# The scaled product of three ternary weight matrices moved to GpSimd, with more staging places and the third weight's sums in the first stage, in an attention and ternary feed-forward layer on eight cores

## The reference, cut to what matters

```python
def _weight_quant(w):
    scale = 1.0 / jnp.clip(jnp.mean(jnp.abs(w)), 1e-05)
    wq = jnp.clip(jnp.round(w * scale), -1.0, 1.0) / scale
    return w + jax.lax.stop_gradient(wq - w)
def _bitlinear(x, w):
    return jnp.einsum('bsi,oi->bso', _act_quant(x), _weight_quant(w))
...
qkv = grouped_linear(x, w_qkv, None)            # 8 groups of 128 channels
q, k, v = (qkv[0] * scale, qkv[1], qkv[2])      # 16 heads of 64
attn = jax.nn.softmax(jnp.einsum('bhnd,bhmd->bhnm', q, k), axis=-1)
out = jnp.einsum('bhnm,bhmd->bhnd', attn, v)    # then projected by w_proj
...
x = _layernorm(x + attention(x))
gate = jax.nn.silu(_bitlinear(x, w_gate))       # w_gate, w_up 4096 x 1024
up = _bitlinear(x, w_up)
x = _layernorm(x + _bitlinear(gate * up, w_down))   # w_down 1024 x 4096
```

## Time and profile before

| | us |
|---|---|
| median of 3 runs | 1290.41 (1288.22 to 1415.11) |
| profiled execution, its own time | 1290.59 |
| its span, slowest core (core 4) | 1289.0 |
| spans of the eight cores | 1278.8 to 1289.0 |
| busy in it: PE, DVE, ACT, POOL | 1149.7, 911.7, 616.9, 117.4 |

### The profile page before, as it was taken

How to read it: one execution, slowest core, us unless ns; L and a number is a source line. 1 busy time by engine, 2 the same in 40 slices (tenths; PEclk the granted TensorE clock), 3 DMA queues, 4 the chain that set the end, 5 groups by cost and what they waited for, 6 DMA issues and landing times.

```text
span 1289.0 us, 17877 instructions; the slowest of 8 cores (1278.8 to 1289.0 us)
## 1 busy us (share of the span) xinstructions
PE 1149.7 (89%) x6465; PEld 455.1 (35%) x6502; DVE 911.7 (71%) x1797; ACT 616.9 (48%) x679; POOL 117.4 (9%) x146
## 2 busy tenths in 40 slices
PE   3888998884898886599999999999999999999997
PEld 0333333321333222233333333333444444444443
DVE  4878889977899874474664547353789777977774
ACT  3798998884454487555555555554011111110110
POOL 1222112220001000010010001000000000000000
PEclk8999999997899898799999999999999999999999
DMA  8999934569799757242323223020523333233313
GB/s 237 307 326 316 325 102 158 176 195 318 239 250 226 208 138 241 90 92 65 92 70 78 86 39 117 5 70 1 145 89 81 89 82 99 72 89 66 82 34 82
DMA packets 129031, 179.74 MB, mean 139 GB/s; under 512 B 90033, under 2 KB 90801, under 8 KB 128946
## 3 DMA queue, kind: packets, MB, share of 16 engines
q1 hardware_dynamic: 120050, 149.52, 41.1%
q0 software_dynamic: 8896, 29.08, 7.4%
HBM read 127.41 MB, written 30.93 MB: 123 GB/s over the span
## 4 chain that ended last, share of the span: by engine, by line
PE 66%; DVE 13%; DMA 12%; ACT 5%; issue 4%; SPq 0%; POOL 0%; DVEq 0%; ACTq 0%; POOLq 0%
PE ps L802 32%; PE ps L897 16%; DMA stage<-wu 6%; PE ps L553 6%; PE ps L571 6%; PE ps L578 5%; ACT P L559 4%; DMA stage<-wd 3%; DVE asum L417 2%; DVE G L434 1%; ACT G L430 1%; DMA stage<-wg 1%; DMA stage<-xT 1%; DVE wgq L440 1%; DVE h L814 1%
## 5 line engine op out<-in xcount | busy, mean ns | idle before, releaser
L559 ACT ACTIVATE P<-ps 128x1024 bf16<-128x1024 f32 x512 | 492.5, 1021 | 236.6 <-PE ps L553 234.9
L808 ACT ACTIVATE T<-ps,tsc 128x512 f32<-128x512 f32 x128 | 88.0, 687 | 376.3 <-PE ps L802 330.5
L802 PE MATMUL ps<-wgq,xqT 128*128 128x512 fp8e4 x1024 | 249.2, 383 | 15.2 <-DVE hm L840 5.2
L802 PE MATMUL ps<-wuq,xqT 128*128 128x512 fp8e4 x1024 | 250.0, 384 | 8.7 <-DVE h L814 8.6
L897 PE MATMUL ps<-wdq,hqT 128*128 128x512 fp8e4 x1024 | 229.9, 380 | 1.3 <-DVE wdq L440 1.3
L571 PE MATMUL ps<-P,onesb 128*64 128x512 bf16 x1024 | 206.3, 399 | 14.2 <-DVE DT L594 14.2
L553 PE MATMUL ps<-Q,K 64*128 64x512 bf16 x1024 | 175.0, 389 | 44.1 <-ACT P L559 34.7
L578 PE MATMUL ps<-P,V 128*64 128x512 bf16 x1024 | 199.9, 386 | 0.9 <-DVE RC L598 0.5
L802 PEld LDWEIGHTS ps<-wuq,xqT 128*128 128x128 bf16 x1024 | 97.0, 99 | 142.0 <-issue 35.3
L802 PEld LDWEIGHTS ps<-wgq,xqT 128*128 128x128 bf16 x1024 | 95.8, 98 | 144.9 <-issue 39.9
L897 PEld LDWEIGHTS ps<-wdq,hqT 128*128 128x128 bf16 x1024 | 97.4, 98 | 129.8 <-issue 17.8
(11 more groups left out here) (95 smaller groups left out, 703.1 us busy)
## 6 DMA issues: line engine op xcount, KB each, us to landing
stage<-wu SPq DMA_DIRECT2D x64, 512.0 KB, 12.2
stage<-wd SPq DMA_DIRECT2D x58, 512.0 KB, 5.5
stage<-wg SPq DMA_DIRECT2D x42, 512.0 KB, 19.1
stage<-xT SPq DMA_DIRECT2D x16, 512.0 KB, 13.6
XB<-x SPq DMA_DIRECT2D x16, 512.0 KB, 5.3
xp_s<-XB SPq DMA_DIRECT2D x16, 512.0 KB, 2.6
Y<-xp_s SPq DMA_DIRECT2D x16, 512.0 KB, 4.3
y<-Y SPq DMA_DIRECT2D x16, 512.0 KB, 2.6
```

What stands on the lines that cost most here:

```text
L559: exp_tok[i] = act.do(lambda e: e.activation(P_sb[i % 4][:, :], bank(sb, 2), AF.Exp, bias=-C0, scale=0.125), pv_tok.get(i - 4), t)
L802: tp = pe.do(lambda e, ic=ic, w=w, bk=bk: e.matmul(bank(bk), xqT[b][:, ic, :], W_sb[w][:, 8 * q + ic, sl], start=(ic == 0), stop=(ic == 7) ...
L808: ta = act.do(lambda e: e.activation(T[:, :], bank(gb), AF.Tanh, bias=0.0, scale=tsc[:, t:t + 1]), tp, T_free[k], sc_tok[t])
```

## The change

The first operation of all 96 ternary tiles goes to GpSimd: times the scale, times 1.0, into 8-bit integers that saturate. VectorE does the limits for all of them, as before, but two tiles later in its queue than the product is put into GpSimd's, so four `G1` buffers are used. In the credit, a tile now costs 0.75 (the limit alone). w_up's first 16 ternary tiles use 12 places, 0 to 7 and 18 to 21. The sums of w_down use places 0 to 7, with no hold; only places 22 to 29 are held, until step 230 of the first stage. The pace of the first stage is 0.62 throughout (0.3 from step 242, as before). The first stage has 252 steps in place of 256, and the other 4 go into the second. `AT` has two buffers, and its loads are issued one tile earlier. `RB` has one buffer.

```diff
-    AT = alloc("AT", [128, 8, 128], BF16)[0]
+    AT = [alloc(f"AT{i}", [128, 7, 128], BF16)[0] for i in range(2)]
-    G1 = [alloc(f"G1{i}", [128, 1024], I8)[0] for i in range(2)]
+    G1 = [alloc(f"G1{i}", [128, 1024], I8)[0] for i in range(4)]
-    RB = [alloc(f"RB{i}", [128, 512], F32)[0] for i in range(2)]
+    RB = alloc("RB", [128, 512], F32)[0]
...
-    order += [("tern", 1, k, k % 8, True) for k in range(16)]
-    order += [("tern", 0, k, k % 8, True) for k in range(22, 24)]
+    ring = list(range(8)) + [18, 19, 20, 21]
+    order += [("tern", 1, k, ring[k % 12], True) for k in range(16)]
+    order += [("tern", 0, 22, 4, True), ("tern", 0, 23, 5, True)]
...
-    ring = [0, 1] + list(range(22, 30))
-    order += [("sum", 2, k, ring[n % 10], True) for n, k in enumerate(rest)]
+    order += [("sum", 2, k, n % 8, True) for n, k in enumerate(rest)]
...
-            if hold[0] and w == 2:
+            if hold[0] and s_ >= 22:
                 return
...
             if kind == "sum":
+                while second:
+                    yield limit()
...
-            if w == 2:
-                t = act.do(lambda e, w=w, src=src, b=b: e.activation(
-                    G1[b][:, :], src[:, :], AF.Identity, bias=0.0, scale=wst[:, 8 * w + 2:8 * w + 3]),
-                    g1_tok[b], t_stat[w], load_tok.get(o))
-            else:
-                t = dve.do(lambda e, w=w, src=src, b=b: e.tensor_scalar(
-                    G1[b][:, :], src[:, :], wst[:, 8 * w + 2:8 * w + 3], 1.0, ALU.mult, ALU.min),
-                    g1_tok[b], t_stat[w], load_tok.get(o))
+            t = pool.do(lambda e, w=w, src=src, b=b: e.tensor_scalar(
+                G1[b][:, :], src[:, :], wst[:, 8 * w + 2:8 * w + 3], 1.0, ALU.mult, ALU.mult),
+                g1_tok[b], t_stat[w], load_tok.get(o))
             used(o, t)
+            second.append((w, k, b, t))
+            if len(second) > 2:
+                yield limit()
...
+    def limit():
+        w, k, b, t = second.popleft()
+        g1_tok[b] = dve.do(lambda e: e.tensor_scalar(
+            W_sb[w][:, k, :], G1[b][:, :], -1.0, 1.0, ALU.max, ALU.min, saturate=False),
+            t, t_qkv_last[0] if w == 2 else None)
+        t_tern[(w, k)] = g1_tok[b]
+        return 0.75, None
...
-            RC[:, :].rearrange("r (k c) -> r k c", c=1).broadcast_to([128, 16, 32])), t2, u_free[b])
+            RC[:, :].rearrange("r (k c) -> r k c", c=1).broadcast_to([128, 16, 32])), t2, u_free[1 - b])
...
-            pace = 0.55 if 0 not in t_red else 0.75 if ast[0] < 230 else 0.95
+            pace = 0.62
...
-    for i in range(0, 256, 2):
+    for i in range(0, 252, 2):
...
             load_at(0)
+            load_at(1)
+        if i == 230:
+            hold[0] = False
+            for s_ in range(22, 30):
+                stage_tok[s_] = t_qkv_last[0]
+            load_more()
...
-    load_at(1)
-    hold[0] = False
...
-                if t + 1 != 8:
-                    load_at(t + 1)
+                if t + 2 < 16 and (t + 2) // 8 == t // 8:
+                    load_at(t + 2)
...
         elif kind == "X":
-            need_weights(2, 31)
+            if t == 0:
+                for k in range(32):
+                    need_weights(2, k)
```

More of the change, by code:

```diff
@@ L145, in build @@
     AO7 = alloc("AO7", [128, 1024], BF16)[0]
-    AT = alloc("AT", [128, 8, 128], BF16)[0]
-    blo, _ = alloc("blo", [128, 1024], BF16, at=off[0] - 2048)
+    AT = [alloc(f"AT{i}", [128, 7, 128], BF16)[0] for i in range(2)]
+    blo, _ = alloc("blo", [128, 1024], BF16, at=off[0] - 3584)
     b3, _ = alloc("b3", [128, 1024], BF16)
@@ L328, in build @@
     t_red = {}
-    g1_tok = [None, None]
+    g1_tok = [None] * 4
     g1_n = [0]
@@ L425, in weight_ops @@
                 continue
-            b = g1_n[0] % 2
+            b = g1_n[0] % 4
             g1_n[0] += 1
-            if w == 2:
-                t = act.do(lambda e, w=w, src=src, b=b: e.activation(
-                    G1[b][:, :], src[:, :], AF.Identity, bias=0.0, scale=wst[:, 8 * w + 2:8 * w + 3]),
-                    g1_tok[b], t_stat[w], load_tok.get(o))
-            else:
-                t = dve.do(lambda e, w=w, src=src, b=b: e.tensor_scalar(
-                    G1[b][:, :], src[:, :], wst[:, 8 * w + 2:8 * w + 3], 1.0, ALU.mult, ALU.min),
-                    g1_tok[b], t_stat[w], load_tok.get(o))
-            used(o, t)
[L438 to L443, removed]
+            t = pool.do(lambda e, w=w, src=src, b=b: e.tensor_scalar(
+                G1[b][:, :], src[:, :], wst[:, 8 * w + 2:8 * w + 3], 1.0, ALU.mult, ALU.mult),
+                g1_tok[b], t_stat[w], load_tok.get(o))
+            used(o, t)
+            second.append((w, k, b, t))
+            if len(second) > 2:
+                yield limit()
+        while second:
+            yield limit()
+    second = deque()
+    def limit():
[5 more added lines that the diff above has]
+        return 0.75, None
     later = []
@@ L600, in norm @@
         t3 = dve.do(lambda e: e.transpose(
-            RB[b][:, :].rearrange("r (k c) -> r k c", c=32),
-            RC[:, :].rearrange("r (k c) -> r k c", c=1).broadcast_to([128, 16, 32])), t2, u_free[b])
+            RB[:, :].rearrange("r (k c) -> r k c", c=32),
+            RC[:, :].rearrange("r (k c) -> r k c", c=1).broadcast_to([128, 16, 32])), t2, u_free[1 - b])
         def mult():
@@ L606, in mult @@
                 ao7_tok[qc] = u_free[b] = pool.do(lambda e: e.tensor_tensor(
-                    AO7[:, 512 * qc:512 * qc + 512], U_sb[b][:, :], RB[b][:, :], ALU.mult),
+                    AO7[:, 512 * qc:512 * qc + 512], U_sb[b][:, :], RB[:, :], ALU.mult),
                     pool.sem.tok(), t3, u_done_of[u], ao7_free[qc])
@@ L611, in mult @@
             t4 = u_free[b] = pool.do(lambda e: e.tensor_tensor(
-                AO[b][:, :], U_sb[b][:, :], RB[b][:, :], ALU.mult),
+                AO[b][:, :], U_sb[b][:, :], RB[:, :], ALU.mult),
                 pool.sem.tok(), t3, u_done_of[u], ao_free[b])
@@ L685, in load_at @@
         b = t % 2
-        atl_tok[t] = pool.dma(sem(f"atl{b}"), AT[:, 0:7, :], at_s[t, :, 0:7, :], at_free[0],
+        atl_tok[t] = pool.dma(sem(f"atl{b}"), AT[b][:, :, :], at_s[t, :, 0:7, :], at_free[b],
                               *[at_tok[(p, t // 4)] for p in range(7)])
@@ L723, in proj_half @@
             g = 4 * hf + j
-            src = AT[:, g, :] if g < 7 else AO7[:, 128 * (t % 8):128 * (t % 8) + 128]
+            src = AT[b][:, g, :] if g < 7 else AO7[:, 128 * (t % 8):128 * (t % 8) + 128]
             tp = pe.do(lambda e, g=g, j=j, src=src: e.matmul(
@@ L735, in proj_half @@
             return
-        at_free[0] = tp
+        at_free[b] = tp
         if t == 3 or t == 7:
@@ L951, in build @@
             load_at(0)
+            load_at(1)
[4 more added lines that the diff above has]
+            load_more()
         if i in (242, 244):
             proj_half(0, i // 2 - 121)
+            if i == 244:
+                load_at(2)
         att_weights(None if i < 242 else 0.3)
@@ L964, in build @@
         bgstep(1.0)
-    load_at(1)
-    hold[0] = False
-    for s_ in range(22, 30):
-        stage_tok[s_] = t_qkv_last[0]
-    load_more()
     gu_on[0] = True
@@ L1005, in need_weights @@
                 run_later(force=True)
+                while totals:
+                    totals.pop()(7)
+            assert not wdone[0] or (w, k) in t_tern
     for kind, t in seq:
@@ L1017, in build @@
                 load_at(8)
+                load_at(9)
             proj_half(t, 0)
@@ L1031, in build @@
                 if t == 0 and oc == 7:
+                    while 2 not in t_red:
+                        credit[0] = 1.0
+                        weight_step(credit)
                     hqT_alias[0] = [stage_tok[6], stage_tok[7]]
```

## The result

The changed kernel takes 1312.9 us (median of 4 runs, 1310.6 to 1313.4) against 1289.3 for the kernel before: a ratio of 1.0187, 95% interval 1.0175 to 1.0200. The forecast was 1258, 2.5% faster. The loss is just inside the range, and has the other sign. One of the four runs of the kernel before (1415.1 us) was in the slower state that some executions of every kernel here show, and is left out of the ratio.

A forecast was written before the change was run, and what follows sets the result against it. The prediction took TensorE to set the end after 548 us, with gains only in the differently bound stretches before; +30 - 24 - 9 - 31 + 2 = -32 us from 1290.6 gave about 1258 us, range 1225 to 1315.

The forecast's parts named there:

- P1 no longer waits: -24: Start of the second stage: with AT in two buffers, tile 1's projection no longer waits for its AT load, saving 24 us.
- what is late next is xqT of tile 0 ... no wait of size: After P1: the next late input is xqT of tile 0, its VectorE work issued before step 252, so no sizeable wait.
- P1 to GU2: Second stage, three blocks and two projections: less VectorE work makes it 160 us in place of 169, -9.
- First stage: Attention's 252 steps: late sums (3 us) and product-limit exclusion (34 us) move its end from 302 to 332, +30.
- 163 + 3: First stage: the last of 64 sums at 163 us by pace, plus 3 us of delay because DMA is full.
- my bound of 12: First stage: upper end of the sums' delay, put at 3 us (0 to 12), DMA being full until 160 us.
- Wait before D0: Before the first w_down matmul: all of w_down is ready early, so the wait goes, -31 us (526 to 495).
- Four steps: Four attention steps moved out of the first stage cost 4 x 0.6 us of TensorE, +2 us.
- B: Rival: GpSimd's product is dear, 1.9 us, delaying first stage and second-stage products; 1331 us, 3% slower; chance 0.18.
- A: Rival: no exclusion of size between GpSimd and VectorE; the ternary stretch costs 7 us, not 34; 1231 us; chance 0.2.
- C: Rival: gain given back by larger first-stage delays and GU0 to GU1 still bound by VectorE; 1284 us; chance 0.17.

The follow-up runs named there:

- Experiment 4: The kernel before with AT in two buffers, its loads issued one tile earlier, and RB in one buffer, nothing else of the change: 1287.0 us, ratio 1.0002.
- experiment 3: The changed kernel with places 22 to 29 released at the end of the first stage (the late release) in place of step 230: 1299.2 us.
- Experiment 10: w_down's sums on ScalarE: in a row, on the kernel before with two AT buffers, 1311.9 us; one by one, second stage only, on experiment 6, 1282.7 us.
- experiment 5: Kernel before, two AT buffers, w_gate and w_up products on GpSimd: 1285.8 us. Changed kernel, products on VectorE and ScalarE, places 22 to 29 released late: 1288.6 us.
- experiment 1: A small kernel without the layer: eight GpSimd products and eight VectorE limits, alone, together, and with sums; one run, 97.4 us, no layer time.
- experiment 6: The changed kernel with places 22 to 29 released at the first stage's end and a ternary tile counted 1.1 in place of 0.75: 1281.4 us, ratio 0.9943.

## Why the prediction was wrong

**The step that failed is the one on AT: "P1 no longer waits: -24", with "what is late next is xqT of tile 0 ... no wait of size".** It measured +4 and is 28 us off; the step after it adds 18, and the two turn the sign. Experiment 4 shows the term at 0 in the kernel before: xqT of tile 0 landed only at 322.9, 4.5 us before GU0. VectorE's backlog that I named as the cause of GpSimd's late product was as much the cause of a late xqT, and I removed one of two waits of nearly equal length. In the changed kernel it came worse: the early release put loads ahead of the transfer of xqT (experiment 3, 13 us). I had checked the loads of AT against GpSimd's queue, and not SyncE's queue, where the change puts 34 loads ahead of that one transfer.

**P1 to GU2, -9, measured +9.** I took VectorE's 147 of 169 us for the bound and counted its work. Experiment 10 takes 30 us of that work away and gains 4 us in the stretch and none in the time. In the changed kernel VectorE is busy for only 86 of 110 us from 370 to 480. The chain there goes through products, transfers of w_down (18.9 us of GpSimd's idle time) and VectorE's limits, with the tanh products queued among them; so a part of the 31 us saved before D0 is paid here, one tile at a time. Of the 9 us, some 4 are there with the old engines and the late release too (171.4 us, experiment 5), and some 4 come with the products on GpSimd (175.2, experiment 3). The cores of one execution differ by up to 5 us in this stretch, so the parts are rough.

**First stage, +30, measured +39.** The mechanism was right, and nearly its rates: exclusion (experiment 1), 1.63 us for a tile in a row against 1.72 by the sum, 1.86 with all that comes between against 1.8, and the product's price, 1.11 against 1.07. The reading of two pairs of rows was enough for that. By the cited section of the Trainium skill ("SBUF — State Buffer", section "SBUF: two separate sides", there under "Who interferes with whom") VectorE's reductions never contend for the shared ports on this chip; the trace agrees, with sums every 1.14 us and products of 1.11 beside them (experiment 1).

That the size came so near is in part luck. Step 252 is over only at 350, not at 332: 18 us late. But the first stage of the kernel before ends at 316 and not at 302, which was step 242: 14 us the other way. Of the 18, ten are sums: the last of the 64 ended at 176 us in place of 163 + 3; DMA was full until 160, at 323 GB/s, and my bound of 12 was the better value. The rest is in the tiles (119 us in place of 115, 75 steps in place of 77). And the exclusion is not the whole of the delay. With both operations on the old engines and the late release P0 is 24 us late (experiment 5), and it is GpSimd that adds the other 11 or 12 (329.1 to 340.5, and 326.3 to 337.8). The 24 are work moved forward and come back before D0; what is lost for good is the engine's 11 and the transfers' 13 us.

**Wait before D0, -31: right. Four steps, +2:** from D0 on it measured -1; a term of this size can't be told apart.

**Rivals.** B (a dear product) is refuted by 1.11 to 1.13 us, though its 1331 is nearer to the measured time than the forecast. A is refuted by experiment 1. C is the nearest in what happened (the sums' ten us, and GU0 to GU2 no faster), but it has neither the transfer queue nor the late xqT, and says 1284.

**What costs, in the end.** The credit says 0.75 for a tile, which puts one in every 1.27 us, and product and limit need 1.63 together, so the order puts tiles in faster than they can be made; all engines keep the order, and attention is what waits. Counted 1.1, the same kernel with the late release is faster than before by 0.57% (0.41 to 0.74). Why experiment 6 beats the kernel before is shown by stretch and not by part: P0 is 13 us later, GU0 follows it 6 us sooner (19.5 in place of 25.5), and D0 comes 182.0 us after GU0 in place of 198.6, since the kernel before waits 31 us for w_down there; together D0 starts 9 us earlier. Which single part of the change earns this stays open.

## What to carry to other kernels

Before moving work to GpSimd to relieve VectorE, ask whether the partner operations exclude each other; an 8-bit tensor_scalar on VectorE and a product on GpSimd did, for 0.5 of the former's 0.6 us (a float32 one did in the one meeting of the earlier trace rows), while a reduction did not. In a program whose order is fixed by estimated costs, an engine change must change the estimate too: 0.75 against 1.1 was 18 us with the products on GpSimd, and 4 without. When a wait is removed, look up when the next input of the same consumer lands, and look through every queue, SyncE's too, for what the change puts ahead of it. When the profile names an engine as what ended a wait, compare with the landing of the transfer that the instruction needs.

## What was not expected of the hardware

A limit on VectorE could be held for 3.8 us, behind three products in a row (214.49 us; the longest took 4.4), while in the small kernel, with products queued back to back too, each limit got its turn after at most one product (longest 1.53 us). What decides between the two wasn't found. And a transposing transfer of 256 KB, 3.1 us otherwise, took 14.4 behind nine loads and one store of 512 KB that were issued earlier and landed from 356.0 to 368.8. Their 5 MB need 16 us at 327 GB/s, and a part had already moved.
